# A graph layer on one core: stores moved to ScalarE's queue, eight tiles gathered by SP, a semaphore for each gathered unit

## What is computed

```
h = maximum(layernorm(x), 0)
# per edge e
a   = silu(silu(edge_attr_8 @ W1 + b1) @ W2 + b2)
tpw = a @ W3 + b3                       # 4 blocks of 8 x 8 weights
m   = tensor product of h[src[e]] (8 scalars, 8 vectors of 3) with edge_attr_4[e], weighted by tpw
agg = segment_sum(m, dst, 100000) / 4
# per node
h_self = [hs @ Ws, hv @ Wv] / sqrt(8)
out = x + h_self + agg
```

## Time and profile before

| what | value |
|---|---|
| median of 3 runs | 633.53 us (630.18 to 634.61) |
| the profiled execution | 632.85 us |
| its span, first to last instruction | 631.1 us |
| PE / DVE / ACT / POOL busy | 540.0 / 465.1 / 387.5 / 499.6 us |
| granted PE clock, mean | 0.813 of full speed |
| moved by DMA | 34.27 MB |

### The profile page before, as it was taken

How to read it: one execution, slowest core, us unless ns; L and a number is a source line. 1 busy time by engine, 2 the same in 40 slices (tenths; PEclk the granted TensorE clock), 3 DMA queues, 4 the chain that set the end, 5 groups by cost and what they waited for, 6 DMA issues and landing times.

```text
span 631.1 us, 11807 instructions
## 1 busy us (share of the span) xinstructions
PE 540.0 (86%) x2867; PEld 400.6 (63%) x2867; DVE 465.1 (74%) x1125; ACT 387.5 (61%) x1103; POOL 499.6 (79%) x396
## 2 busy tenths in 40 slices
PE   5799999899589998888998988889799889986800
PEld 4698888797446666656666656666476666754700
DVE  4769898776758987877778777787777778857700
ACT  3435655454359775877576675768576777865400
POOL 6747777777777788888888888888888888878886
PEclk9969999899778888888686778887867777887655
DMA  4656666564211122222222222222222222222222
GB/s 126 188 192 195 200 196 189 179 179 126 82 25 15 13 11 11 11 12 10 11 10 12 11 10 10 12 11 10 11 9 10 10 10 10 8 11 9 10 8 8
DMA packets 52409, 34.27 MB, mean 54 GB/s; under 512 B 35910, under 2 KB 39816, under 8 KB 52360
## 3 DMA queue, kind: packets, MB, share of 16 engines
q0 software_dynamic: 34336, 6.37, 19.4%
q1 hardware_dynamic: 17960, 27.35, 12.8%
q10 hardware_dynamic: 64, 0.00, 0.0%
HBM read 17.59 MB, written 16.08 MB: 53 GB/s over the span
## 4 chain that ended last, share of the span: by engine, by line
POOL 59%; issue 19%; DMA 16%; SPq 3%; PE 2%; DVE 0%; POOLq 0%; ACT 0%; DVEq 0%
POOL out_dram L340 38%; POOL xg L323 21%; DMA out_dram<-sums,idx_i 15%; DMA er_all<-in_edge_attr_dram 1%; PE ps L609 1%; PE ps L594 0%; PE ps L605 0%; SPq L258 0%; DMA wself<-in_L_gnn_Wv_dram 0%; SPq L219 0%; SPq L238 0%; PE ps L579 0%; PE ps L631 0%; SPq L233 0%; SPq L252 0%
## 5 line engine op out<-in xcount | busy, mean ns | idle before, releaser
L340 POOL DMA_INDIRECT out_dram<-sums,idx_i x196 | 305.8, 1560 | 63.0 <-issue 53.1
L323 POOL DMA_INDIRECT xg<-in_x_dram,src_all x191 | 192.8, 1010 | 65.7 <-issue 57.3
L650 PE MATMUL ps<-w3blk,x 128*128 128x512 f32 x196 | 142.5, 819 | 0.0
L704 PE MATMUL ps<-msg,eq 128*128 128x32 f32 (+1 forms) x980 | 126.6, 288 | 1.7 <-DVE msg L1041 1.1
L704 PEld LDWEIGHTS ps<-msg,eq 128*128 128x128 f32 x980 | 126.4, 210 | 2.2 <-DVE msg L1041 1.6
L1021 DVE TENSOR_REDUCE red<-prod 128x128 f32<-128x1024 f32 x49 | 97.7, 1994 | 0.1
L486 ACT ACTIVATE dsq<-ps,dcol 128x512 f32<-128x512 f32 x196 | 87.3, 538 | 0.2 <-PE ps L662 0.2
L474 ACT ACTIVATE sums<-ps 128x132 f32<-128x132 f32 x49 | 13.7, 280 | 116.0 <-POOLq L350 94.5
L650 PEld LDWEIGHTS ps<-w3blk,x 128*128 128x128 f32 x196 | 47.2, 255 | 44.5 <-issue 40.9
L508 ACT ACTIVATE eq<-dsq,onecol 128x384 f32<-128x384 f32 x147 | 73.4, 519 | 0.0
L605 PEld LDWEIGHTS ps<-ones_g,sqT 128*128 128x128 f32 x392 | 53.4, 204 | 19.5 <-issue 17.7
(11 more groups left out here) (102 smaller groups left out, 817.3 us busy)
## 6 DMA issues: line engine op xcount, KB each, us to landing
xin<-in_x_dram SPq DMA_DIRECT2D x48, 256.0 KB, 3.3
out_dram<-oc SPq DMA_DIRECT2D x48, 256.0 KB, 2.1
xg<-in_x_dram SPq DMA_DIRECT2D x552, 0.1 KB
out_dram<-sums,idx_i POOLq DMA_INDIRECT x196, 3.1
xg<-in_x_dram,src_all POOLq DMA_INDIRECT x191, 2.4
er_all<-in_edge_attr_dram SPq DMA_DIRECT2D x1, 780.0 KB
sh_all<-in_edge_attr_dram SPq DMA_DIRECT2D x1, 390.0 KB
xin<-in_x_dram SPq DMA_DIRECT2D x1, 192.0 KB
```

Of the source, the lines that this page charges most:

```text
L323: pool.indirect_dma_start(xg[:, t * D:(t + 1) * D], None, x, bass.IndirectOffsetOnAxis(ap=src_all[:, t:t + 1], axis=0)).then_inc(signal, 16)
L340: pool.indirect_dma_start(out, bass.IndirectOffsetOnAxis(ap=idx_i[:, k % NS, a:a + 1], axis=0), sums[:, k % NS, a * DR:a * DR + D], None, ...
L650: pe.matmul(o, x2[:, k // 2 % 2, j * P:(j + 1) * P], w3blk[:, :], start=True, stop=False)
L704: m = pe.matmul(psSUM[:, a * DR:a * DR + n], eq[:, k % 2, o:o + P], msg[:, k % 2, b, 0:n], start=(b == a), stop=(b == a - 1 and (a < BT - ...
```

## The change

1. SP no longer stores. ACT's queue issues all 50 stores: in its node step of chunk c it waits for `o_done` of chunk c - 4 and issues that store behind the root of chunk c - 2; the last two stand behind the first activation of the edge stage.
2. SP's program in the node stage is written out without a device loop: the load of chunk c, and for c = 12 to 47 four of its single-row gathers behind it (144 rows). The register loads take 32 row numbers at a time.
3. `RT` goes from 5 to 8: SP gathers tiles 188 to 195 (936 rows), POOL tiles 0 to 187. Tiles 188 and 189 belong to the unit before the last.
4. Each of the 12 early units has its own semaphore, and POOL waits for no `feat_sum` any more.
5. DVE's node steps are written out without a device loop, and wait for constants. The tail load of `dst_i` stands ahead of the loads of row numbers.

```
-    GT, GL, GA, RT = 10, 7, 157, 5
+    GT, GL, GA, RT = 10, 7, 157, 8
...
-        gathered = [sem(f"gathered{i}") for i in range(3)]
+        gathered = [sem(f"gathered{i}") for i in range(EARLY)]
...
-            def store(c, base):
-                sp.wait_ge(s["o_done"], c + 1)
-                v, p, n = rows(out, c, base)
-                sp.dma_start(v, oc[0:p, base % XS, 0:n]).then_inc(stored[base % XS], 16)
...
-            node_pass(0, True)
-            with sp.Fori(1, DLOOP - 1) as i:
-                node_pass(i, False)
...
+            late_rows = iter([(t, p) for t in range(G1, T + 1) for p in range(P if t < T else TAIL)])
+            nodes = []
+
+            def gather_rows(count):
+
+                for t, p in itertools.islice(late_rows, count):
+                    if p % 32 == 0:
+                        o = (t - G1) * P + p
+                        w = min(32, (P if t < T else TAIL) - p)
+                        _, numbers = nc.values_load_multi_w_load_instructions(
+                            row_i[0:1, o:o + w], engines=[mybir.EngineType.SP], min_val=0, max_val=N - 1,
+                            skip_runtime_bounds_check_because="src holds rows of x")
+                        nodes[:] = numbers
+                    sp.dma_start(xg[p:p + 1, t * D:(t + 1) * D], x[ds(nodes[p % 32], 1), :])\
+                      .then_inc(gathered_row[t - G1], 16)
+
+            for c in range(XS, NCH):
                 load_x(c, c)
...
+                if c == 12:
+                    sp.wait_ge(row_loaded, 16 * RT)
+                if 12 <= c < FULL:
+                    gather_rows(4)
+            gather_rows(P * RT)
...
-                signal = gathered_late[(t - GF) // GL] if t >= GF else gathered[t // GT % 2 if t >= GT else 2]
+                signal = gathered[t // GT] if t < GF else gathered_late[(t - GF) // GL]
...
-            for n in range(EARLY):
-                if n >= 3:
-                    pool.wait_ge(s["gsum_done"], n - 1)
-                for t in range(n * GT, (n + 1) * GT):
-                    gather(t)
-            for t in range(GF, GA):
+            for t in range(GA):
                 gather(t)
...
+            def store(c, base):
+                act.wait_ge(s["o_done"], c + 1)
+                v, p, n = rows(out, c, base)
+                act.dma_start(v, oc[0:p, base % XS, 0:n]).then_inc(stored[base % XS], 16)
...
+                if base >= 4:
+                    store(c - 4, base - 4)
...
             mlp_one(0, 0)
+            for c in range(NCH - 2, NCH):
+                store(c, c)
             mlp_in(1, 1)
...
-                    odd = base % 8 == 2
-                    if base < 8:
-                        dve.wait_ge(gathered[2], 16 * GT)
-                    else:
-                        dve.wait_ge(gathered[odd], i * (16 * GT))
+                    dve.wait_ge(gathered[n], 16 * GT)
```

More of the change, by code:

```diff
@@ L14 @@
+import itertools
 import numpy as np
@@ L262, in _ @@
             sp.dma_start(sh_all[0:TAIL, T * 4:T * 4 + 4], edge_sh[T * P:E, :]).then_inc(s["sh_loaded"], 16)
+            sp.wait_ge(s["dst_pad"], 1)
+            sp.dma_start(dst_i[0:TAIL, T:T + 1], dst[T * P:E].rearrange("(n a) -> n a", a=1)).then_inc(s["dst_loaded"], 16)
             for t in range(G1, T + 1):
@@ L267, in _ @@
                     sp.dma_start(row_i[:, (t - G1) * P:(t - G1) * P + n], rows_of).then_inc(row_loaded, 16)
-            sp.wait_ge(s["dst_pad"], 1)
-            sp.dma_start(dst_i[0:TAIL, T:T + 1], dst[T * P:E].rearrange("(n a) -> n a", a=1)).then_inc(s["dst_loaded"], 16)
             sp.dma_start(out[N:N + BT * P, :].rearrange("(p r) d -> p (r d)", p=P), spare0[:, :]).then_inc(s["spare_stored"], 16)
[L273 to L280, removed]
@@ L282, in _ @@
-            node_pass(0, True)
-            with sp.Fori(1, DLOOP - 1) as i:
-                node_pass(i, False)
-            for k in range(DBODY):
-                c = (DLOOP - 1) * DBODY + k
-                store(c - XS, c - XS)
-                load_x(c, c)
[L289 to L305, removed]
+            late_rows = iter([(t, p) for t in range(G1, T + 1) for p in range(P if t < T else TAIL)])
@@ L817, in loaded_count @@
             def loaded_count(c, base):
-                if isinstance(c, int):
-                    return 16 * (c // XS + 1)
-                return loop["i"] * (16 * DBODY // XS) + 16 * ((base - DBODY) // XS + 1)
+                return 16 * (c // XS + 1)
             def node_rstd(c, base):
@@ L842, in node_add @@
                                   ALU.add).then_inc(s["o_done"], 1)
-            loop = {}
             def store_count(c, base):
-                if isinstance(c, int):
-                    return 16 * (c // XS)
-                return loop["i"] * (16 * DBODY // XS) + 16 * ((base - DBODY) // XS)
+                return 16 * (c // XS)
             def gathered_rows(t0, w):
@@ L860, in feat_centre @@
                 dve.wait_ge(s["gsum_done"], n + 1)
-                if not isinstance(n, int) or n > 0:
+                if n > 0:
                     dve.wait_ge(s["h_done"], n)
@@ L882, in feat_scale, with node_step @@
                                          op0=ALU.max, op1=ALU.mult).then_inc(s["h_done"], 1)
-            def node_step(c, base, i):
-                n = 2 * i + base % 8 // 4 - 1
+            def node_step(c):
+                base, n = c, (c - 6) // 4 if c % 4 == 2 else (c - 4) // 4
                 ahead = base % 2 == 1 and base + 2 < NCH
@@ L923, in _ @@
             for k in range(DBODY):
-                node_step(k, k, 0)
+                node_step(k)
                 if k == 6:
@@ L940, in _ @@
                               trash[:, :].rearrange("p (a t) -> p a t", a=1).to_broadcast([P, NQ, BT]), ALU.subtract)
[L941 to L946, removed]
+            for c in range(DBODY, NCH + 2):
+                node_step(c)
             def coefs(u, k, w=UT):
```

## The result

Over 20 runs each the kernel before takes 632.46 us and the changed one 628.14 us (median); the ratio of the runs is 0.9948, with a 95% interval of 0.9928 to 0.9969. A later set gave 632.42 and 627.81, ratio 0.9916 (0.9887 to 0.9945). Ratios and intervals leave out disturbed executions, such as the 637.79 us of the changed kernel in the later set (granted clock 0.695, where the others have 0.81 to 0.84); medians take in all. So the change is worth 3 to 5 us, 0.5 to 0.8%. The forecast was -9.8 us and 623.4 us: the right direction, and about twice the size.

A forecast was written before the change was run, and what follows sets the result against it. POOL's program, its instructions plus one stall, was taken to bound the kernel: -6.36 us for the wait and -3.47 us for three gathers make -9.83 us, other parts 0, so 623.4 us, range 620 to 628.5.

The forecast's parts named there:

- What bounds the kernel: Whole kernel: POOL's instructions plus one stall set the time; everything else counts only where it makes POOL wait.
- -6.36 us: POOL's early gathers: the 6.66 us pause for DVE's sum of unit 1 becomes the usual 0.30 us.
- rival D: Gathers moved into the pause get dearer beside loaded DMA engines, 0.02 us each, taking back 3.2 us: 626.2 us; 8%.
- -3.47 us: Edge-stage rounds: three gathers leave POOL, saving 1.157 us each (rounds of 7.628 instead of 8.785 us).
- My bounds of 1.0 to 1.32 us: Edge-stage rounds: least and most saved by each gather taken from POOL, so 3.0 to 4.0 us for three.
- Stores on ACT's queue at 0: Node stage: 50 store issues fit ACT's idle gaps of 0.74 and 1.51 us, so they cost 0.
- the node stage's margin: Node stage: 23 us of delay in all stay hidden from POOL, 0.58 us per step over 40 steps.
- rival A: SP's row gathers are late; at 0.55 us per row they end 18 us too late, 641 us; 5%.
- rival C: Node stage: at 0.5 us per row one DMA engine fills up, costing 14 us, 637 us; 3%.
- rival B: Before the first scatter: late batch 0 or stores keep it near 216.8, 630 us, 9%; hard form 640 us, 3%.
- SP's margin: SP's queue: last rows end at 537 to 543 us, before their use, with 18 to 24 us in hand.
- The rule weighed: Node stage: single rows all run on one DMA engine, 2.4 of 2.77 us per step, so the sum stays 623.

The follow-up runs named there:

- front_all: Changed kernel with all of POOL's gathers ahead of the first scatter (`GA` 157 to 188): 638.07 us, ratio to the kernel before 1.0112.
- one_input: Changed kernel with DVE's add reading the unscaled product in PSUM, so the node output's scaling is left out: 625.66 us, ratio to the kernel before 0.9917.
- psum_scale_b: Changed kernel, computing everything, with the scaled product left in PSUM for DVE's add: 625.26 us, ratio to the kernel before 0.9895.
- both_b: Changed kernel with the scaled product left in PSUM and three gathers moved from the front into rounds (`GA` 154): 622.48 us, ratio to before 0.9874.
- sem_only: Kernel before with a semaphore per early unit, POOL's nine waits gone and DVE's node steps written out: 630.42 us, ratio to before 0.9977.
- waitback: Changed kernel with POOL's nine waits for DVE's sums put back: 630.44 us, ratio to the kernel before 0.9987.
- rt5: Changed kernel with `RT` back at 5, so POOL gathers three tiles more: 629.73 us, ratio to the kernel before 0.9956.
- sp_store_b: Changed kernel with the 50 stores back on SP's queue: 626.58 us, ratio to the kernel before 0.9929.

## Why the prediction was right and wrong

*What bounds the kernel: right.* POOL, its issue and the landings that it waits for are over 90% of the chain in all thirteen profiles of the table, and the edits that changed POOL's program by several us (front_all, one_input, psum_scale_b, both_b) moved the time the same way.

*"-6.36 us" for the wait: wrong in size, the first cause of the miss.* The number was true for the profiled execution and not for the kernel. The pause goes with where TensorE's granted clock falls in the first 50 us; in three profiles of the kernel before it was 6.36, 2.34 and 0.42 us, 3.0 in the mean. I read the pause as POOL waiting for DVE and did not ask why DVE's sum of unit 1 was at 47.46. Edited alone, the wait is worth 2.0 us (sem_only) or 2 to 3 (waitback), not 6.36. The rows between 30 and 40 us, with a clock of 0.51, are where I should have looked.

*"The gathers may not be as cheap" (rival D, 8%): happened in this profile, but is not the change's doing.* The extra was 11.9 us against 9.0, just about the 0.02 us per gather that the rival priced. But the rival blamed loaded DMA engines, and one_input shows DVE's operands instead (7.1 with the DMA as it was). Over repeated profiles the extra is 9.0 to 10.5 before and 9.3 to 11.9 in the variants without the wait that leave DVE's operands alone (7.1 with the stall back). It comes from which gathers happen to begin during DVE's two-operand instructions, and how early in them. That mechanism is shown; that the change raised it in the mean is not.

*"-3.47 us" for three gathers: the second mis-sized term.* They are worth 1.9 us by rt5 (629.73 against 627.81), and in the two first profiles even less: from the first scatter to the last it is 410.67 us before and 410.23 after, 0.44 less. A round gains 0.98 (8.795 - 7.819) rather than 1.157, 2.9 us for three; but the fifteen other rounds without a gather lose 0.14 each against the 7.679 before, 2.1 us, and the thirty with one lose 0.3 in the sum. My bounds of 1.0 to 1.32 us excluded the right value by little, but I had bounded the round that loses a gather only, and took the others to stay as they are. I had also left the round up to batch 48 with its wait of 1.21 us out of the mean (7.628 instead of 7.679).

*What the two corrections make.* -3.0 for the wait and -1.9 for the gathers: -4.9, against -4.3 and -4.6 measured in the two sets. That it comes so near is in part luck: the first term is the mean of three stalls between 0.42 and 6.36, the second is known to 1.2 us, and by sem_only the wait is worth anything up to 3.5 us.

*Stores on ACT's queue at 0, the node stage's margin, SP's rows in time (rival A), one engine filling up (rival C), the stall moving (rival B): as forecast.* On the slow chip rival A came true. What the stores' move bought is SP's margin, which the time doesn't show (sp_store_b). A store took 0.34 us of ACT's queue, beside its activations; the first indices were 22 us early; rows took 0.48 us each and ended 19 us before their use. In the node stage SP did fall behind for some steps: each read of 32 row numbers holds its queue for 3 us (load at 61.49, next row at 64.91). The loads' lead hides that: between 15 and 170 us neither PE nor DVE waits for `xin`. The rule weighed stands in the Trainium skill's page under "Why a DMA increments its semaphore by 16 and not by 1", not in the section that I named. No run shows on which DMA engine a row runs, but the trace of the changed kernel has 12 ns in the mean for packets of 128 bytes on SP's queue, far less than the 0.08 to 0.16 us that I allowed for.

*What stays open.* Behind the last gather the kernel before has rounds of 7.68, 7.66 and 7.75 us in its three profiles and sem_only of 7.76, counted up to batch 48 in each; the nine profiles of the changed kernel and what was made from it have 7.80 to 7.93, rt5's 7.84 among them. (The table stops at batch 47 and so leaves out, where the last gather stands ahead of batch 33, a wait of 1 us that the others have in it; that is 0.03 to 0.05 us of the difference.) SP's rows at that time are excluded (rt5, front_all), and so are the number of SP's tiles (rt5) and the stores' queue (sp_store_b, 7.85). Why more scatters land late was not found. Nor was what stops the computing engines on the slow chip.

## What to carry to other kernels

A pause in one profile is a sample: before pricing its removal, look for what made the releaser late, and whether that (a granted clock, a landing) is the same in other executions. If POOL's indirect DMAs set the time, look at what VectorE reads beside them: a gather that begins during an instruction with two operands in SBUF waits for its end. Moving one operand of a 0.69 us add to PSUM took 3 to 4 us off the gathers and 2 to 3 off the time, more than half of what the whole change gave. Leave a queue of late rows its margin: on the slow chip SP's late rows held POOL for 20.65 us. And place gathers where a wait for landings covers them: 0.96 us in a round, 1.20 or more ahead of it.

## What the runs showed of the hardware

- An indirect gather of 128 rows takes POOL 0.95 us. One that begins while DVE works with two SBUF operands ends 0.82 us behind the end of that instruction (762 of 816 such gathers, within 0.02 us), so up to 1.47 us was seen beside one instruction of 0.63 or 0.69 us and 1.76 where several follow one another. Beside reductions, or operations with an operand in PSUM, it isn't lengthened (0.12 us in the sum of 35 to 90 gathers at most).
- In every kernel a fixed place of POOL's program waits about 1 us: ahead of the first scatter of the 15th round behind the last gather (batch 48 before with 1.21, 0.99 and 1.06 us; batch 45 in the changed kernel with 1.05; batch 15 in front_all with 1.01). It follows the program, not the data or the time. Its cause was not tried.
- The kernel before took 765 us on one chip and 630 to 634 in every other set. In its node stage there PE, ACT and DVE stood still together for up to 18 us at a time, while packets of 2 KB took nearly as long as in the first profile (98 and 93 ns in the mean). The cause was not looked for.
